# A chain of four attention and feed-forward layers: the place of one weight slab's sum of squares in the slot order of the first attention

## The reference, cut to what matters

```python
q = rmsnorm((ln(x) @ q_proj_w.T) per head of 128, q_norm_w)      # 32 heads
k = rmsnorm((ctx @ k_proj_w.T) per head of 128, k_norm_w)        # 8 key heads, each for 4 query heads
v = (ctx @ v_proj_w.T) per head of 128
attn = softmax(q k^T / sqrt(128) + mask)                         # 64 queries x 64 keys of one batch entry
x = x + (attn v, heads side by side) @ o_proj_w.T
```

## Time and profile before

| what | us |
|---|---|
| median of 3 runs | 2261.2 (2258.11 to 2262.14) |
| the profiled execution | 2254.16 |
| its span, first to last instruction | 2252.3 |
| mean granted TensorE clock | 0.98 |
| first attention's projections and units | about 49 to 580 of the span |
| TensorE busy, ScalarE, VectorE, GpSimd (share of the span) | 93%, 52%, 59%, 24% |

### The profile page before, as it was taken

One profiled execution on the slowest core, in us unless ns is written; L12 is line 12 of the kernel. 1 busy time (PEld: TensorE's weight loads), 2 busy tenths in 40 slices (PEclk: granted clock), 3 DMA queues, 4 the chain that ended last, 5 costly groups with the idle time before them and its releaser, 6 DMA issues.

```text
span 2252.3 us, 40195 instructions
## 1 busy us (share of the span) xinstructions
PE 2100.5 (93%) x13704; PEld 1150.1 (51%) x13704; DVE 1332.3 (59%) x2699; ACT 1160.9 (52%) x3008; POOL 538.0 (24%) x936
## 2 busy tenths in 40 slices
PE   6799999999899799999999999998879799999998
PEld 3456565566554344555555555555434355555564
DVE  6677676676750556666656666555642466666664
ACT  5666666666312335555555555543332566666651
POOL 4233232332300412222222222212310122222221
PEclk9899999999989999999999999999979999999999
DMA  3122121220111113222233322211200133323211
GB/s 127 59 65 58 46 63 41 62 60 18 58 81 54 51 61 87 74 82 81 70 92 73 85 80 68 73 36 48 95 36 1 53 80 80 75 75 79 58 51 38
DMA packets 181412, 144.91 MB, mean 64 GB/s; under 512 B 158122, under 2 KB 166570, under 8 KB 171234
## 3 DMA queue, kind: packets, MB, share of 16 engines
q1 hardware_dynamic: 180770, 142.40, 22.4%
q10 hardware_dynamic: 448, 0.03, 0.0%
HBM read 102.29 MB, written 2.10 MB: 46 GB/s over the span
## 4 chain that ended last, share of the span: by engine, by line
PE 65%; DVE 14%; ACT 12%; issue 6%; POOL 1%; DMA 1%; DVEq 0%; ACTq 0%; POOLq 0%; SPq 0%
PE bank L84 18%; PE bank L85 18%; PE bank L86 18%; ACT m_E L496 3%; PE bank L1887 3%; PE bank L1533 2%; DVE m_Sm L929 2%; ACT m_arena L368 2%; DVE m_x L980 2%; ACT m_arena L475 2%; DVE m_A L974 1%; PE bank L1433 1%; DVE m_nmax L946 1%; ACT m_arena L467 1%; ACT m_arena L466 1%
## 5 line engine op out<-in xcount | busy, mean ns | idle before, releaser
L875 DVE TENSOR_TENSOR m_arena<-bank,m_arena 128x512 f16<-128x512 f32 x320 | 221.3, 691 | 475.8 <-ACT m_arena L475 475.2
L84 PE MATMUL bank<-m_input_parts,m_arena 128*128 128x512 f16 x1088 | 417.1, 383 | 9.3 <-DVE m_arena L875 2.6
L85 PE MATMUL bank<-m_input_parts,m_arena 128*128 128x512 f16 x1088 | 416.4, 383 | 0.0
L86 PE MATMUL bank<-m_input_parts,m_arena 128*128 128x512 f16 x1088 | 416.0, 382 | 0.0
L992 POOL TENSOR_TENSOR m_E<-m_E,m_rinv 128x512 f32<-128x512 f32 (+1 forms) x192 | 172.3, 898 | 803.1 <-DVE m_rinv L960 803.1
L496 ACT ACTIVATE m_E<-m_Sm,m_nmax 128x64 f32<-128x64 f32 (+1 forms) x512 | 185.4, 363 | 284.4 <-DVE m_nmax L950 148.7
L475 ACT ACTIVATE m_arena<-bank 128x512 f16<-128x512 f32 x320 | 189.3, 592 | 234.8 <-PE bank L86 234.4
L86 PE MATMUL bank<-m_wo_t,m_A 128*128 128x512 f16 x768 | 291.8, 380 | 0.0
L84 PE MATMUL bank<-m_wo_t,m_A 128*128 128x512 f16 x768 | 291.8, 380 | 0.0
L85 PE MATMUL bank<-m_wo_t,m_A 128*128 128x512 f16 x768 | 291.6, 380 | 0.0
L84 PE MATMUL bank<-m_arena,m_input_parts 128*128 128x128 f16 (+1 forms) x768 | 188.2, 276 | 7.4 <-DVE m_arena L880 6.6
(11 more groups left out here) (281 smaller groups left out, 4169.1 us busy)
## 6 DMA issues: line engine op xcount, KB each, us to landing
m_raw<-a_q SPq DMA_DIRECT2D x24, 1024.0 KB, 5.0
m_raw<-a_o SPq DMA_DIRECT2D x24, 1024.0 KB, 5.0
m_raw<-a_k SPq DMA_DIRECT2D x9, 1024.0 KB, 5.4
m_raw<-a_v SPq DMA_DIRECT2D x9, 1024.0 KB, 5.1
m_bias_in<-bias SPq DMA_DIRECT2D x64, 128.0 KB, 2.1
m_arena<-f_w SPq DMA_DIRECT2D x3, 1024.0 KB, 7.4
m_PT<-m_split SPq DMA_TRANSPOSE x174, 3.0
m_x<-x SPq DMA_DIRECT2D x2, 1024.0 KB, 7.0
```

Of the source, the lines that this page charges most:

```text
L84: pe.matmul(out, lhs[0], rhs[0], start=first, stop=False)
L85: pe.matmul(out, lhs[0], rhs[1], start=False, stop=False)
L86: return pe.matmul(out, lhs[1], rhs[0], start=False, stop=last)
L875: ins = dve.tensor_tensor(self.dest(name, part, 1), self.shaped(name, bank[m % 2][:, :]), self.dest(name, part, 0), ALU.subtract)
```

## The change

In the first attention, in the second and the sixth slot of each period, the event `w_sum` moves from ahead of the first projection tile to behind it and behind `rinv`. It stays in the same slot, keeps its number in the sequence of bank 7's uses, and no instruction is added or taken away. It moves on the three engines that have a part in it: TensorE's one matmul from ahead of tile Q2 to between Q2 and Q3; VectorE's read of the total from ahead of Q2's differences to behind the reciprocal; GpSimd's chain of factors from ahead of the product that normalises the probabilities to behind it. It concerns 14 slots: slot 5 of the opening, slots 1 and 5 of periods 1 to 6, slot 1 of period 7.

```diff
@@ -184,7 +184,8 @@
                 out.append(("f_norm", slot))
             if normed == 2:
                 out.append(("k_inv", slot // 4))
-            if made is not None:
+            behind = self.layer == 0 and slot % 4 == 1
+            if made is not None and not behind:
                 out.append(("w_sum", made, misc))
                 misc += 1
             if normed == 3 and made is not None:
@@ -206,6 +207,9 @@
                     out += [("k_read_hi", misc - 1, slot // 4), ("k_read", misc - 1, slot // 4)]
             if ok(b):
                 out.append(("rinv", b))
+            if made is not None and behind:
+                out.append(("w_sum", made, misc))
+                misc += 1
             if squared is not None:
                 out.append(("w_squares", squared))
             if ok(b - 1) and not self.by_dma(t, b - 1):
```

## The result

The changed kernel takes **2266.5 us** as the median of 15 runs (2260.6 to 2268.9); the kernel before, beside it, took 2260.1 us (15 runs, 2254.7 to 2262.3). The ratio is **1.0031, 95% interval 1.0021 to 1.0040**: slower by some 7.0 us, between 4.7 and 9.1. The forecast was 2265.9, slower by 4.7: the difference forecast is the lower end of what was measured.

The account below looks back on a forecast made before the run. The prediction took the loop through ScalarE, VectorE and GpSimd as the bound: 13 slots x 0.36 us gave 4.7 us more, put on the median of 2261.2 us for 2265.9 us, range 2259.5 to 2273.5.

Parts of the forecast that it names:

- What bounds the kernel: Periods 1 to 6: the loop through ScalarE, VectorE and GpSimd bounds; TensorE, 93% busy, runs ahead and waits.
- TensorE: Slots 1 and 5: the 1.12 us wait goes, Q2 gains about 0.6 us, Q3 starts as before; gain at the end 0.
- the 0.5 us wait that was named as a sign: Ahead of K0, TensorE would still wait some 0.5 us for VectorE's second difference of Q2.
- VectorE: Read of the total, behind the reciprocal, hides in 0.70 us of idle time ahead of Q3's difference; cost 0.
- GpSimd: Normalisation gains 0; factors come late, delaying ScalarE's conversion 0.48 us and VectorE's low part 0.36 us per slot.
- the sign named for it: GpSimd's idle time ahead of the normalisation would stay near 1.7 us.
- The knife edge: GpSimd's product making w_scale starts at 317.32, 0.03 us ahead of VectorE's difference of Q3; taken as not extended.
- The port's rival: VectorE's Q3 difference gets its inputs before GpSimd's product; low part 0.92 us late, 12.0 us more, 2273.2 us; chance 0.25.
- The opening and period 7: Opening's slot 5 costs 0, its conversion coming long after the normalisation; period 7's slot 1 costs the same 0.36 us.
- The sum: Whole kernel: 12 slots of periods 1 to 6 and slot 1 of period 7, 13 x 0.36 = 4.7 us more.
- TensorE's waits count: Rival at the start of Q2: removing TensorE's 16.1 us of waits makes the kernel faster, 2245.1 us; chance 0.07.
- The delay is taken up: Rival: unseen room between the late low part and the next exponentials absorbs the delay; no change, 2261.2 us; chance 0.18.

Follow-up runs that it names:

- the seven experiments: Variants of the kernel before: w_sum's engine parts moved separately or together, one GpSimd product added, or ScalarE's squares moved late; ratios from 0.9884 to 1.0058.
- TensorE alone: Against the kernel before, only TensorE's matmul of w_sum moved behind the first tile, VectorE's and GpSimd's parts staying ahead; ratio 1.0004, 2260.7 us.

## Why the prediction was right, and where it was off

**What bounds the kernel.** Right. TensorE is busy for 93% of the span and its 12 waits were worth nothing (34.31 against 34.33 us), while 0.36 us on the loop showed in full in each half period.

**TensorE.** Right in both places and in their sum: waits of 0.61 and 0.58 us ahead of Q2 and Q3, where its rows give 0.49 and 0.70. Missed was slot 2's sum. I had said that only Q3 is queued behind the moved sum, and had looked at the queue but not at bank 7's next user. It waits 0.91 us, and K0 no longer has the 0.5 us wait that was named as a sign; TensorE and VectorE moved together show that this costs nothing.

**VectorE.** Right. The read is hidden: Q3's difference still waits 0.65 us where it waited 0.70.

**GpSimd.** Right. The normalisation gained nothing, though the sign named for it, an idle time that stays near 1.7 us, did not hold: with the factors gone from ahead of it, it reads 9.45. The factors came late. The conversion starts 0.97 us behind the copy ahead of it (320.05 to 321.02) instead of 0.48 (316.58 to 317.06), so it is 0.49 us late for a forecast 0.48; the low part waits and a half period is 0.36 us longer, forecast 0.36. The knife edge fell as I took it: the product began at 320.79, 0.03 us ahead of the difference at 320.82, and took its normal 0.19 us. The next power, begun inside it, took 0.99 instead of 0.54 us, which nothing waits for; 12 powers are longer so, by 0.45 us each, more than the whole 4.4 us by which GpSimd's busy time grew.

That the product came first by 0.03 us was luck, and the prediction had said that it couldn't vouch for it. The port's rival was a real mechanism with the wrong start time; 0.27 us more of work made it happen. It had the product end 0.04 us behind the difference and the low part 0.92 us late. In that experiment the product ended 0.05 us behind it, and the low part came 2.80 us behind the difference's start (323.35 to 326.15) instead of 1.86, 0.94 late.

**The opening and period 7.** The opening was put at nothing. There the last factor's product met the same difference (0.51 us instead of 0.19) and the low part of the k slab, which had no wait, shows one of 0.15 us; from slot 5 to the next period's first exponentials the trace grows by 0.2 us. In period 7 the low part came 0.98 us later, with a wait of 0.89 us for the conversion; by the last exponentials of the first attention 0.62 of that were taken up again. That leaves 0.36 us, as forecast, but by another way: there was room behind a delay that was larger.

**The sum.** 12 x 0.37 + 0.2 + 0.36 = 5.0 us in the trace, forecast 4.7. Read directly it is the same: the two traces stand 1.00 us apart at the normalisation of the opening's slot 5, ahead of the first factors moved, and 5.98 at the last exponentials of the first attention. The measured 7.0 has 4.7 to 9.1 as its interval, and GpSimd's part alone came out at 1.0023, 5.2 us.

The profiled pair differs by 8.5 us, but the first attention doesn't hold all of it. From the last bias of the third attention to the last residual sum of the fourth the profile of before took 2207.7 - 1574.4 = 633.3 us, the one of after 636.8, and the seven experiments, which change nothing there, 636.2 to 641.1. Most of that lies in its first part, up to the first exponentials of the fourth attention: 202.2 us before, 204.8 after, and about 205 or 209 in the experiments. Before, the granted clock was 0.93 there and TensorE busy for 170.1 us; after, 0.91 and 173.9. So the profile of before was a lucky one in that stretch; what makes the 209 of four experiments isn't shown. Whether the change costs 5 or 7 us can't be told from these runs. That the median of 2266.5 lies 0.6 us from the 2265.9 forecast is luck too: the 4.7 was put on a median of three runs, 2261.2, and the 15 runs beside the changed kernel gave 2260.1.

**The rivals.** "TensorE's waits count" fell with TensorE alone. "The delay is taken up" fell with the half periods. The port didn't act on the product in the changed kernel, but was shown to act when it starts a quarter of a microsecond later.

## What to carry to other kernels

A wait on the busiest engine is worth what ends behind it: ask what the next instruction waits for, and the one behind that, before it is counted as a gain. When an event is shared by several engines, move each engine's part by itself; here the parts of TensorE and VectorE were free and GpSimd's cost the whole loss. And look for the piece on the loop that stands just ahead of an idle time on its own engine; moving it, together with the part of the change that is free, gave 1.2%.

## What the runs showed of the hardware

A one-column product of GpSimd begun 0.03 us ahead of a VectorE instruction with two SBUF inputs took 0.19 us; begun 0.24 us inside one it took 0.49 us. Two more products begun inside one, 0.25 us (in the changed kernel's opening) and 0.29 us (with TensorE's and VectorE's parts moved), took 0.51 and 0.45 us; all three ended 0.05 or 0.06 us behind VectorE's instruction. A power of GpSimd begun 0.11 us inside such an instruction took 0.99 us, one outside 0.54. VectorE's instruction took 0.70 us where the product had begun 0.03 us ahead of it, and 0.68 where it began 0.24 us inside it. So an addition of 0.27 us on GpSimd cost 0.58 us on the loop.
